# The query's spectrum copied early, and a new order of all five engines' lists, in a two-layer attention and low-rank expert kernel

## What is computed

```python
def _autocorrelation(Q, K, V):          # layer 0, heads of 128 channels
    qf = jnp.fft.fft(q, axis=2)
    kf = jnp.fft.fft(k, axis=2)
    corr = jnp.fft.ifft(qf * jnp.conj(kf), axis=2).real
    w, idx = jax.lax.top_k(corr.transpose(0, 1, 3, 2), 9)
    w = jax.nn.softmax(w, axis=-1)
    ...                                  # sum of w_i * v[min(idx_i + pos, L - 1)]
x = x + _autocorrelation(_layernorm(x), ctx, ctx)
x = x + _L0_ffn_ref(_layernorm(x), W_base, b_base, W_router, A_stack, B_stack)  # base + top 2 of 8 experts, rank 16
x = x + _L1_xattn_ref(_layernorm(x), ctx, Wq, bq, Wk, bk, Wv, bv, Wo, bo)       # window of 16, 8 heads of 16
x = x + _L1_ffn_ref(_layernorm(x), A, B, Wr)                                    # top 2 of 4 experts, rank 16
```

## Time and profile before

| | us |
|---|---|
| median of 3 runs (lowest, highest) | 1823.69 (1823.42, 1826.07) |
| the profiled execution, its own time | 1823.51 |
| its span, from the first to the last instruction | 1821.7 |
| busy in the span: PE, DVE, ACT, POOL | 1704.5, 1571.8, 1131.7, 903.1 |
| mean granted TensorE clock | 0.976 |
| `c_attention_residual` (line 1251), 32 times: first and last start | 151.5, 1802.4 |

### The profile page before, as it was taken

One profiled execution on the slowest core, in us unless ns is written; L12 is line 12 of the kernel. 1 busy time (PEld: TensorE's weight loads), 2 busy tenths in 40 slices (PEclk: granted clock), 3 DMA queues, 4 the chain that ended last, 5 costly groups with the idle time before them and its releaser, 6 DMA issues.

```text
span 1821.7 us, 48202 instructions
## 1 busy us (share of the span) xinstructions
PE 1704.5 (94%) x19296; PEld 1081.3 (59%) x19296; DVE 1571.8 (86%) x4758; ACT 1131.7 (62%) x1929; POOL 903.1 (50%) x933
## 2 busy tenths in 40 slices
PE   4699999999999999999999999999999999999975
PEld 2356566666656666655666665666665666666553
DVE  7779889889889888988988898988898998889853
ACT  5257656666765666665666676566666666657642
POOL 2355554555554545555455555444555545555432
PEclk8899999999999999999999999999999999999995
DMA  6033322243332233332223343223443322333220
GB/s 225 24 59 71 59 53 51 52 71 71 71 59 48 50 58 71 71 66 48 51 50 71 71 71 59 50 50 55 71 71 71 47 49 50 69 71 59 31 30 24
DMA packets 549359, 111.37 MB, mean 61 GB/s; under 512 B 531088, under 2 KB 531344, under 8 KB 548624
## 3 DMA queue, kind: packets, MB, share of 16 engines
q1 hardware_dynamic: 549136, 108.30, 31.8%
HBM read 57.94 MB, written 16.78 MB: 41 GB/s over the span
## 4 chain that ended last, share of the span: by engine, by line
PE 56%; DVE 20%; ACT 10%; POOL 8%; issue 5%; DMA 0%; DVEq 0%; SPq 0%; POOLq 0%; ACTq 0%
PE pb L602 18%; PE pc L677 8%; ACT q_diag L877 6%; POOL prob L1424 4%; POOL rest L1422 4%; PE pa L523 4%; ACT v_im L777 3%; PE pa L495 3%; PE pa L524 3%; PE pa L496 3%; PE pa L497 3%; PE pb L591 3%; DVE rows_c L1251 2%; PE pa L563 2%; DVE rest L1105 2%
## 5 line engine op out<-in xcount | busy, mean ns | idle before, releaser
L602 PE MATMUL pb<-w_base_h,even_words 128*128 128x512 f16 x1024 | 324.8, 379 | 0.0
L1431 POOL TENSOR_TENSOR p_hl<-sc,p_hl 128x512 f16<-128x512 f32 x128 | 164.1, 1282 | 219.9 <-ACT p_hl L777 219.9
L1458 POOL TENSOR_TENSOR sc<-sc,sc_rec 128x512 f32<-128x512 f32 x128 | 134.4, 1050 | 266.2 <-DVE sc_rec L1238 266.2
L877 ACT ACTIVATE q_diag<-sc,own 128x512 f32<-128x512 f32 x384 | 244.3, 710 | 3.1 <-DVE sc L1149 3.1
L602 PE MATMUL pb<-w_base_l,even_words 128*128 128x512 f16 x512 | 193.9, 379 | 0.0
L486 PE MATMUL pa<-xn_a,tab 128*128 128x512 f32 x384 | 180.7, 607 | 3.8 <-ACT xn_a L777 3.8
L677 PEld LDWEIGHTS pc<-sc_t,v_diag 128*128 128x128 f16 x6144 | 170.2, 97 | 20.6 <-DVE sc_t L1245 5.9
L677 PE MATMUL pc<-sc_t,v_diag 128*128 128x32 f16 x6144 | 173.9, 177 | 5.5 <-DVE sc_t L1245 5.5
L655 PE MATMUL pc<-k_h,q_diag 128*128 128x32 f16 x2048 | 169.0, 177 | 0.0
L656 PE MATMUL pc<-k_l,q_diag 128*128 128x32 f16 x2048 | 168.4, 177 | 0.0
L657 PE MATMUL pc<-k_h,q_diag 128*128 128x32 f16 x2048 | 168.4, 177 | 0.0
(11 more groups left out here) (165 smaller groups left out, 4658.4 us busy)
## 6 DMA issues: line engine op xcount, KB each, us to landing
x_a<-in_x SPq DMA_DIRECT2D x32, 512.0 KB, 5.8
x_res<-in_ctx_in SPq DMA_DIRECT2D x32, 512.0 KB, 5.6
x_res<-in_x SPq DMA_DIRECT2D x32, 512.0 KB, 3.7
v_diag<-even_words SPq DMA_DIRECT2D x128, 128.0 KB, 4.9
v_diag<-p_hl SPq DMA_DIRECT2D x128, 128.0 KB, 5.0
out<-rows_c SPq DMA_DIRECT2D x32, 512.0 KB, 2.6
v_diag<-in_base_w SPq DMA_DIRECT2D x4, 1024.0 KB, 10.1
q_diag<-in_ra SPq DMA_DIRECT2D x1, 544.0 KB, 13.8
```

The source lines that it names most:

```text
L602: mm(pb[:, h, :], rows[:, cols], weights[:, j, h * HALF:(h + 1) * HALF], start=(j == 0 and m == 0), stop=False)
L877: nc.scalar.activation(q_diag[:, blocks, head * QB:(head + 1) * QB], q_hl.rearrange("p (n t) -> p n t", t=QB)[:, blocks], ACT.Copy, scale= ...
L1431: g_.tensor_tensor(part[:, :, :, LO], sc[:, g % 2, :, :], part[:, :, :, HI], ALU.subtract)\
L1458: g_.tensor_tensor(sc[:, g % 2, :, :], sc[:, g % 2, :, :], sc_rec[:, blocks].unsqueeze(2).to_broadcast([P, GB, KEYS]), ALU.mult)\
```

## The change

The copies take the query's spectrum: `a_values` becomes `a_query_crossed` and `a_query_same`, which read `pa` 2:4 and wait for `mm_q`; `a_product` multiplies them with the context's spectrum in `pa` 0:2 and waits for `mm_ctx`; the sign of one table is turned for it. `a_context_long(b, 0)` then waits for the copies instead of the products.

```diff
-    corr_2 = np.concatenate([sin, -sin])
+    corr_2 = np.concatenate([-sin, sin])
...
-        v_placed = signal("v_placed", 16 * 2 * PAIRS)
+        v_placed = [signal(f"v_placed{n}", 16 * PAIRS) for n in range(2)]
...
                 if n == 0:
-                    pe.wait_ge(prod_q.sem, prod_q.after(b))
-                    pe.wait_ge(prod_q2.sem, prod_q2.after(b))
+                    pe.wait_ge(v_out.sem, v_out.after(b))
...
+                if part == 1:
+                    last.then_inc(mm_base.sem, 1)
...
-            def a_values(b):
-                act.wait_ge(mm_ctx.sem, mm_ctx.after(b))
+            def a_query_crossed(b):
+                act.wait_ge(mm_q.sem, mm_q.after(b))
...
-                    copy(v_im[rows, :], pa_lo[other, :]).then_inc(v_out.sem, 1)
+                    copy(v_im[rows, :], pa[other, 2:4, :].rearrange("p n t -> p (n t)")).then_inc(v_out.sem, 1)
+            def a_query_same(b):
+                act.wait_ge(mm_q.sem, mm_q.after(b))
...
-                copy(v_re[:, :], pa_lo).then_inc(v_out.sem, 1)
+                copy(v_re[:, :], pa_hi).then_inc(v_out.sem, 1)
...
-                dve.wait_ge(mm_q.sem, mm_q.after(b))
+                dve.wait_ge(mm_ctx.sem, mm_ctx.after(b))
...
-                v.tensor_tensor(c1[:, :], pa_hi, v_re[:, :], ALU.mult).then_inc(prod_q.sem, 1)
+                v.tensor_tensor(c1[:, :], pa_lo, v_re[:, :], ALU.mult).then_inc(prod_q.sem, 1)
...
+                    dve.wait_ge(x1_out.sem, x1_out.after(b, h + 1))
+                    v.bn_stats(bn[1][:, h, :], x_b[:, cols]).then_inc(ln_bn[1].sem, 1)
...
-                    dve.wait_ge(mm_ffn[0].sem, mm_ffn[0].after(b))
+                    dve.wait_ge(mm_base.sem, mm_base.after(b))
...
+                if g >= 2:
+                    dve.wait_ge(pl_out.sem, pl_out.after(b, g - 1))
```

More of the change, by code:

```diff
@@ L460, in step @@
             def step(i, live):
+                if live(4):
+                    place_values(i - 4, 1)
+                if live(5):
+                    store(i - 5)
                 if live(1):
[L462 removed]
+                    next_ctx(i - 1)
                 if live(2):
[L464 to L470 removed]
+                    load_x_res(i - 2)
+                if live(0):
+                    next_x(i)
                 if live(3):
[L472 to L474 removed]
+                    place_values(i - 3, 0)
+            for i in range(BATCH + 5):
                 step(i, during(i))
@@ L975, in step @@
                     a_transposed(i - 1, 1)
+                if first(i - 1):
+                    split_weights(range(SPLITS + 1, WEIGHTS_SPLIT))
                 if live(2):
@@ L1281, in step @@
             def step(i, live):
-                if live(2):
-                    c_subtract(i - 2, 2)
-                if live(1):
-                    gates(i - 1, 0, pb, E0)
+                if live(1):
+                    a_lead(i - 1)
+                if live(3):
+                    c_subtract(i - 3, 2)
+                    c_transpose(i - 3, 0)
+                    c_sums(i - 3, 2)
+                    c_inverse(i - 3, 2)
+                    c_transpose(i - 3, 1)
+                    c_scores(i - 3, 3)
+                    c_subtract(i - 3, 3)
@@ new lines, in step @@
+                if live(2):
+                    gates(i - 2, 0, pb, E0)
+                    b_keys(i - 2)
+                if live(3):
+                    c_sums(i - 3, 3)
+                    c_inverse(i - 3, 3)
+                    c_transpose(i - 3, 2)
+                if live(1):
+                    a_ninth(i - 1)
+                    a_softmax(i - 1)
+                if first(i - 1):
+                    split_weights(range(SPLITS))
+                if live(3):
+                    c_transpose(i - 3, 3)
@@ new lines, in step @@
+                if live(3):
+                    c_norm_rows(i - 3)
+                if live(1):
+                    a_products(i - 1, 2)
+                    a_products(i - 1, 3)
+                if first(i - 1):
+                    split_weights(range(SPLITS, WEIGHTS_SPLIT))
+                if live(2):
+                    b_queries(i - 2)
+                    b_values(i - 2, 1)
+                if live(3):
+                    choose(i - 3, 1, pc, E1)
+                    gates(i - 3, 1, pc, E1)
@@ L1299, in step @@
+                if live(1):
+                    a_residual(i - 1)
+                    variance(i - 1, 1)
+                if live(3):
+                    c_result(i - 3, 0)
+                if live(1):
+                    b_norm_rows(i - 1, 1)
                 if live(0):
-                    a_ninth(i)
+                    a_product(i)
                 if live(2):
-                    c_transpose(i - 2, 3)
+                    c_scores(i - 2, 0)
+                    c_subtract(i - 2, 0)
+                if live(1):
+                    b_features(i - 1, 0)
@@ L1334, in step @@
-                if live(2):
-                    gates(i - 2, 1, pc, E1)
-                if live(0):
-                    a_residual(i)
-                if live(2):
-                    c_result(i - 2, 0)
-                if live(0):
-                    b_norm(i, 1, x1_out)
-                    variance(i, 1)
-                if live(1):
-                    c_scores(i - 1, 0)
-                if live(0):
-                    b_norm_rows(i, 1)
-                if live(1):
-                    c_subtract(i - 1, 0)
@@ new lines, in step @@
+                if live(1):
+                    a_normalise(i - 1)
+                if live(2):
+                    b_bias(i - 2)
+                if first(i - 2):
+                    clear_values()
+                if live(2):
+                    root(i - 2, 2)
+                if live(3):
+                    root(i - 3, 3)
+                if live(0):
+                    root(i, 0)
+                    ctx_low(i)
+                if live(1):
+                    a_sum(i - 1, 0)
+                    a_sum(i - 1, 1)
```

296 lines of the change are left out of this document (136 added, 160 removed).

## The result

The changed kernel takes **1953.28 us** (1951.97 to 1953.82, four runs) against 1824.28 (1823.42 to 1826.07, four runs) of the kernel before on the same chip: a ratio of 1.0705, 95% interval 1.0689 to 1.0721. The forecast was 1872 with a range of 1814 to 1890. The direction was right, the size was not: 129 us longer instead of 48. The profiled execution has a span of 1950.1 us, before it was 1821.7.

What follows compares the result with a forecast made beforehand. PE was taken as nearly full, the circle closing through DVE's residual, copies and products. A step of 53.85 + 0.72 + 0.87 = 55.44, +1.71, gives +49.6 over 29 steps: 1823.6 + 49.6 − 1 = 1872 us, range 1814 to 1890.

Steps and rivals of the forecast that it cites:

- Both port blocks: POOL's running instruction holds up DVE: a head block before b_norm_rows of x_b, +0.72 a step; ctx_low before c_norm_rows, +0.87.
- Case C: Rival: both queued POOL head blocks pass before DVE's b_norm_rows of x_b; 1903 us, chance 0.10.
- The exchange: 2.85 us gained by early copies, paid for by c_router 1.45 later and a_query's 1.80, less 0.3: net +0.12 a step.
- Case D: Rival: copies leave the path, root(A,0) comes 0.9 earlier, c_router is not late; step 53.0, 1802 us, chance 0.13.
- +0.87, all on the path: c_norm_rows, held up by ctx_low, ends at 40.05, so c_features starts at 40.8 instead of 39.94: +0.87 a step.
- what would show it right: Signs: L1038 about 1.5 on x_b, 2.5 on rows_c; a_corr distance 55.4; copies off the chain; PE waiting before c_router.
- my two terms: The added times of DVE held up by POOL, at b_norm_rows of x_b (+0.72) and c_norm_rows (+0.87) in each step.
- Start and end: Outside the loop: start −1, with b_norm_rows no longer waiting for the memset (−6.6) among its terms; end about 0.
- The thin margins: PE stays dense from 0 to 30.7: c_transpose(2) at 20.7 for 20.9, vagg_out at 7.6 for 7.8.
- The terms of the new path: Matmul, half residual, bn_stats, variance and root, b_norm_rows, two products to a_corr: 6.9 instead of 9.75, 2.85 gained.
- my own case: The exchange plus both DVE operations held up by POOL, one head block each time at x_b: 1872 us, chance 0.40.

## Why the prediction was off

- **Both port blocks: right, in place and in size.** 1.45 and 2.54 were measured for "about 1.5" and "2.5 or so"; c_norm_rows ended at 40.04 for 40.05. They cost 1.67 a step (55.31 − 53.64) for 1.59. Case C, that two queued blocks of POOL pass before a waiting DVE, fell: 1.45 with two blocks queued is one block, and neither the median (1448 ns) nor the maximum (1450) is above it.
- **The exchange: right within 0.21.** Early query against late c_router came to −0.09 a step (53.64 against 53.73) for a forecast of +0.12; c_router without the block stood at 40.48 for 40.59. Case D's mechanism, root(A,0) early enough and c_router not late, is real, but it needs POOL's old list: 52.85 for 53.0.
- **The step that failed** is the one from "c_features starts at 40.8" to "+0.87, all on the path". I priced the later c_norm_rows as a shift of what follows it, with each PE operation at its duration from the earlier trace rows, so the clock behind the wait was a term put at nothing. Those durations were taken at a granted clock of 1.00. My own account had PE waiting from 37.75 to about 40.1, and under "what would show it right" I even listed "PE waiting before c_router for over 1.5 us"; I did not ask what the rows behind such a wait would cost. They cost 2.81 a step: 0.15 on the transposes, 1.64 on c_router and 1.10 on a_query, less 0.08 in the rest of the step. The two waits of PE at this place add up to 0.44 us in the kernel before, so no row of it showed this price.
- **The sum, closed.** Missing were 135.7 − 49.6 = 86.1 us of the loop. The clock makes 29 × 2.81 = 81.5; the steps above 58.12 add 1694.0 − 29 × 58.12 = 8.5, of the same cause; my two terms and the exchange were 0.13 a step too high, −3.8. Together 86.2.
- **Start and end.** Start −2.9 for −1; end −4.4 for 0. I did not follow up what makes the end shorter. Neither matters beside the loop.
- **The thin margins** between 0 and 30.7 held: no wait of PE showed up before c_attend(2) or b_keys.
- **Slips in the sums.** The terms of the new path from a_aggregate's last matmul to a_corr add up to 6.83, where I wrote 6.9; over 29 steps that is 2 us. And of the waits of PE in a step of the kernel before, which I put mostly between c_router and c_delta, the timeline's brackets give 0.47 there, of some 1.3 in all. Neither bears on the miss.
- **The range.** Its upper end was my own case plus 18 us. A wait of PE of 2.4 us should have been a case of its own.

## What to carry to other kernels

When a change lets TensorE wait somewhere in a loop that it otherwise fills, price what stands behind the wait at the lower clock as well as at the full one. Here a wait of 2.4 us cost another 2.8, and ten idle matmuls in it won 88 us back. Look at GpSimd's list for what can start right behind the small operation that releases a tensor_scalar on VectorE: there the two meet in every step, and where nothing else can be moved, one wait for that tensor_scalar on GpSimd removes it. And take a large reordering apart by engine before judging it: with four of the five lists it was 1.7% faster, with the fifth 7% slower.

## What was unexpected of the hardware

- A VectorE operation that waits for GpSimd's running instruction gets in before GpSimd's next one, though that one has no wait: b_norm_rows took 1.45 with two blocks queued, and the pair of blocks 2.48 where two take 2.04 elsewhere. In the changed kernel (POOL, then DVE):

```profile
812.83 2.48 POOL L1491 TENSOR_TENSOR q_diag<-sc,own 128x512 f32<-128x512 f32 x2
```
```profile
812.97 1.45 DVE L1068 TENSOR_SCALAR xn_b<-x_b,small 128x1024 f32<-128x1024 f32 x1 [0.45 <-POOL small L1441]
```

  812.83 + 1.04 + 0.55 = 814.42, and b_norm_rows ends at 812.97 + 1.45 = 814.42. The second head block is the one that is longer: 1.49 instead of 1.04.
- The granted clock can fall behind a wait as short as 1.01 us, in eight of 29 steps, and can stay up behind one of 1.15, or of 1.47 at another place, in all of them.
- The fall comes late: with the wait of 1.01 over, c_router still ran at the full clock (2.00 us) and only a_query behind it at the lower one (from 2.0 to 2.2 us after the end of the wait). In the changed kernel it came 0.2 to 1.8 us after the end of a wait of 2.36.
